# Two residual convolutions in 32x32 tiles: the relu in two halves, and the first two taps bank pair by bank pair

## What is computed

```python
x = x + relu(conv3x3(group_norm(x), kern) + b)
```

## Time and profile before

| | us |
|---|---|
| median of 3 runs | 4687.26 |
| lowest, highest | 4683.33, 4693.34 |
| profiled execution | 4676.86 |
| its span | 4675.1 |
| PE busy in the span | 4587.9 (98%) |
| DVE busy | 2845.1 (61%) |
| ACT busy | 2199.5 (47%) |
| POOL busy | 1265.0 (27%) |
| granted TensorE clock, mean | 0.997 of full |

### The profile page before, as it was taken

How to read it: one execution, slowest core, us unless ns; L and a number is a source line. 1 busy time by engine, 2 the same in 40 slices (tenths; PEclk the granted TensorE clock), 3 DMA queues, 4 the chain that set the end, 5 groups by cost and what they waited for, 6 DMA issues and landing times.

```text
span 4675.1 us, 288889 instructions
## 1 busy us (share of the span) xinstructions
PE 4587.9 (98%) x138240; PEld 2626.0 (56%) x138240; DVE 2845.1 (61%) x3341; ACT 2199.5 (47%) x2242; POOL 1265.0 (27%) x1093
## 2 busy tenths in 40 slices
PE   5999999999999999999999999999999999999999
PEld 3555555555555555555555555555555555555555
DVE  4656656566566566665666656656656666566564
ACT  4454444544445444444454444444544444445442
POOL 3322322323223222232232322322313223223230
PEclk9999999999999999999999999999999999999999
DMA  3333333333333333333333333333333333333323
GB/s 120 108 120 117 124 121 122 118 122 116 122 121 120 118 119 120 123 118 121 122 119 121 121 120 121 120 121 122 120 121 121 120 125 117 121 122 120 121 91 102
DMA packets 542278, 555.71 MB, mean 119 GB/s; under 512 B 16432, under 2 KB 541104, under 8 KB 541104
## 3 DMA queue, kind: packets, MB, share of 16 engines
q1 hardware_dynamic: 541104, 537.22, 35.0%
HBM read 268.72 MB, written 268.44 MB: 115 GB/s over the span
## 4 chain that ended last, share of the span: by engine, by line
PE 94%; issue 3%; ACT 1%; DVE 0%; ACTq 0%; DVEq 0%
PE ps_y L374 35%; PE ps_y L336 34%; PE ps_x L399 12%; PE ps_x L354 10%; PE ps_y L319 2%; PE ps_x L299 1%; ACT relu L457 1%; ACT relu L454 0%; PE ps_x L309 0%; DVE evens L554 0%; DVE result L571 0%; ACTq L452 0%; DVE pixels L586 0%; DVEq L100 0%; ACT evens L465 0%
## 5 line engine op out<-in xcount | busy, mean ns | idle before, releaser
L374 PE MATMUL ps_y<-odds,scaled 32*32 32x512 f32 x49152 | 1766.8, 600 | 7.9 <-issue 2.2
L336 PE MATMUL ps_y<-evens,scaled 32*32 32x512 f32 x49152 | 1745.3, 598 | 23.6 <-ACT evens L465 8.3
L574 DVE TENSOR_TENSOR odds<-ps_x,relu 128x2048 f32<-128x2048 f32 x256 | 586.8, 2292 | 1110.7 <-PE ps_x L354 842.1
L374 PEld LDWEIGHTS ps_y<-odds,scaled 32*32 32x32 f32 x49152 | 808.0, 103 | 794.2 <-issue 376.4
L336 PEld LDWEIGHTS ps_y<-evens,scaled 32*32 32x32 f32 x49152 | 852.8, 103 | 699.8 <-issue 214.0
L457 ACT ACTIVATE relu<-ps_y,bias 128x2048 f32<-128x2048 f32 x256 | 503.8, 1968 | 1094.3 <-PE ps_y L374 942.7
L280 POOL TENSOR_TENSOR fold<-fold,evens 128x1024 f32<-128x1024 f32 x384 | 845.0, 2200 | 597.3 <-DVE evens L561 309.8
L571 DVE TENSOR_TENSOR result<-ps_x,relu 128x2048 f32<-128x2048 f32 x256 | 586.6, 2292 | 636.4 <-PE ps_x L399 439.2
L454 ACT ACTIVATE relu<-ps_y,bias 128x2048 f32<-128x2048 f32 x256 | 503.7, 1968 | 920.8 <-PE ps_y L336 910.6
L354 PE MATMUL ps_x<-evens,constants 32*32 32x512 f32 x16384 | 786.7, 596 | 0.0
L399 PE MATMUL ps_x<-odds,constants 32*32 32x512 f32 x16384 | 776.2, 604 | 0.0
(11 more groups left out here) (49 smaller groups left out, 1266.7 us busy)
## 6 DMA issues: line engine op xcount, KB each, us to landing
out<-pixels SPq DMA_DIRECT2D x512, 512.0 KB, 3.5
raw<-in_x SPq DMA_DIRECT2D x256, 512.0 KB, 3.9
raw<-in_x SPq DMA_DIRECT2D x128, 576.0 KB, 4.1
raw<-in_x SPq DMA_DIRECT2D x128, 448.0 KB, 3.5
parameters<-in_params SPq DMA_DIRECT2D x2, 96.5 KB, 2.0
constants<-in_consts SPq DMA_DIRECT2D x1, 81.0 KB, 2.0
```

The source lines that it names most:

```text
L336: done = nc.tensor.matmul(ps_y[part, r, :], w0[rows, t * Q:(t + 1) * Q], N0[rows, k:k + EACH, i:i + HQ], start=(t == 0), stop=(t == NTAP - ...
L374: done = nc.tensor.matmul(ps_y[Q * r:Q * (r + 1), q, :], w1[p % 2][Q * q:Q * (q + 1), t * Q:(t + 1) * Q], t1[Q * q:Q * (q + 1), k:k + EACH ...
L574: nc.vector.tensor_tensor(T1[p % 2][:, EACH * f:EACH * (f + 1), 1:1 + H].rearrange("p k (r h) -> p r k h", h=HQ), ps_x[:].rearrange("p r ( ...
```

## The change

ACT's relu becomes two ACTIVATEs of two banks each (banks 0 and 1, then 2 and 3), each of which raises `relued` by one; the sums of layer 0 go to eight columns instead of four. All waits for `relued` are counted anew. PE's order in a round is given by `tile_order`: taps 0 and 1 (LEAD = 2) are done on banks 0 and 1, then taps 0 and 1 on banks 2 and 3, then taps 2 to 5 on all four banks in the old order. The wait for the first relu half stands before the first product on banks 0 and 1, that for the second half before the first product on banks 2 and 3. In the first round of layer 0 the wrap products of taps 0 and 1 come together after the lead. `ps_x`, the small products and the adds stay, the adds waiting for both halves.

```diff
@@ -36,7 +37,10 @@
 HALO0, HALO1 = 2 * (QUADS - 1), QUADS
 ODDS_SUM, ODDS_PAD = 1, 2
 EVENS_SUM = 2
+RELUS = 2
+BANKS = QUADS // RELUS
 HOOK_AFTER = 2
+LEAD = 2
 
 
 def freed(f):
@@ -75,6 +79,15 @@
 
 
 MINI = small_products()
+
+
+def tile_order():
+
+    lead = [(t, bank, other) for i in range(RELUS) for t in range(LEAD)
+            for other, bank in itertools.product(range(QUADS), range(BANKS * i, BANKS * (i + 1)))]
+    rest = [(t, bank, other) for t in range(LEAD, NTAP)
+            for other, bank in itertools.product(range(QUADS), range(QUADS))]
+    return lead + rest
 
 
 def norms_before(y, p):
@@ -122,7 +135,7 @@
         ends = sb("ends", [P, HALVES, 2, C])
         zeros = sb("zeros", [P, PAIRS + 2])
         acc = [sb(f"partial{y}", [P, ROUNDS]) for y in range(2)]
-        acc_relu = sb("partial_relu", [P, ROUNDS])
+        acc_relu = sb("partial_relu", [P, ROUNDS * RELUS])
         sums = [sb(f"sums{y}", [P, 2]) for y in range(2)]
         mom = [sb(f"moments{y}", [P, 2]) for y in range(2)]
         center = [mom[y][:, 0:1] for y in range(2)]
@@ -321,24 +334,26 @@
 
             def conv0(p, f):
                 n = round_of(0, p, f)
-                if n:
-                    pe.wait_ge(relued, n)
                 if f == 0:
                     pe.wait_ge(scaled0, p + 1)
                     pe.wait_ge(padded0, p + 1)
                     pe.wait_ge(halo0, HALO0 * (p + 1))
-                for t in range(NTAP):
+                for t, r, q in tile_order():
+                    if t == 0 and q == 0 and r % BANKS == 0 and n:
+                        pe.wait_ge(relued, RELUS * (n - 1) + r // BANKS + 1)
                     side, i = t // TAPS, t % TAPS
-                    for q in range(QUADS):
-                        for r in range(QUADS):
-                            k = SLOTS * q + EACH * f + side
-                            rows, part = slice(Q * r, Q * (r + 1)), slice(Q * q, Q * (q + 1))
-                            done = nc.tensor.matmul(ps_y[part, r, :], w0[rows, t * Q:(t + 1) * Q],
-                                                    N0[rows, k:k + EACH, i:i + HQ], start=(t == 0),
-                                                    stop=(t == NTAP - 1), skip_group_check=True)
-                    if f == 0 and t < TAPS + 1:
+                    k = SLOTS * q + EACH * f + side
+                    rows, part = slice(Q * r, Q * (r + 1)), slice(Q * q, Q * (q + 1))
+                    done = nc.tensor.matmul(ps_y[part, r, :], w0[rows, t * Q:(t + 1) * Q],
+                                            N0[rows, k:k + EACH, i:i + HQ], start=(t == 0),
+                                            stop=(t == NTAP - 1), skip_group_check=True)
+                    last = r == QUADS - 1 and q == QUADS - 1
+                    if last and f == 0 and t == LEAD - 1:
+                        for tap in range(LEAD):
+                            wrap_pair(tap)
+                    if last and f == 0 and LEAD <= t < TAPS + 1:
                         wrap_pair(t)
-                    if t == HOOK_AFTER and f == 0:
+                    if last and t == HOOK_AFTER and f == 0:
                         if n:
                             pe.wait_ge(added, n)
                         bias_product(0, p)
@@ -359,23 +374,22 @@
             def conv1(p, f):
                 n = round_of(1, p, f)
                 t1 = T1[p % 2]
-                pe.wait_ge(relued, n)
                 if f == 0:
                     pe.wait_ge(scaled1, p + 1)
                     pe.wait_ge(padded1, p + 1)
                     pe.wait_ge(added, round_of(0, p, ROUNDS - 1) + 1)
                     pe.wait_ge(halo1, HALO1 * (p + 1))
                 last_mini = -1
-                for t in range(NTAP):
+                for t, q, r in tile_order():
+                    if t == 0 and r == 0 and q % BANKS == 0:
+                        pe.wait_ge(relued, RELUS * (n - 1) + q // BANKS + 1)
                     side, i = t // TAPS, t % TAPS
-                    for r in range(QUADS):
-                        for q in range(QUADS):
-                            k = EACH * f + side
-                            done = nc.tensor.matmul(ps_y[Q * r:Q * (r + 1), q, :],
-                                                    w1[p % 2][Q * q:Q * (q + 1), t * Q:(t + 1) * Q],
-                                                    t1[Q * q:Q * (q + 1), k:k + EACH, HQ * r + i:HQ * (r + 1) + i],
-                                                    start=(t == 0), stop=(t == NTAP - 1))
-                    if t == HOOK_AFTER:
+                    k = EACH * f + side
+                    done = nc.tensor.matmul(ps_y[Q * r:Q * (r + 1), q, :],
+                                            w1[p % 2][Q * q:Q * (q + 1), t * Q:(t + 1) * Q],
+                                            t1[Q * q:Q * (q + 1), k:k + EACH, HQ * r + i:HQ * (r + 1) + i],
+                                            start=(t == 0), stop=(t == NTAP - 1))
+                    if t == HOOK_AFTER and r == QUADS - 1 and q == QUADS - 1:
                         if f == 0:
                             pe.wait_ge(added, n)
                             bias_product(1, p)
@@ -450,12 +464,15 @@
                 act.wait_ge(y_filled, n + 1)
                 if n:
                     act.wait_ge(added, n)
-                if y == 0:
-                    ins = nc.scalar.activation(R[:], ps_y[:], ACT.Relu, bias=bias[:, 0:1],
-                                               accum_out=acc_relu[:, f:f + 1])
-                else:
-                    ins = nc.scalar.activation(R[:], ps_y[:], ACT.Relu, bias=bias[:, 1:2])
-                ins.then_inc(relued, 1)
+                for i in range(RELUS):
+                    banks = slice(BANKS * i, BANKS * (i + 1))
+                    if y == 0:
+                        at = RELUS * f + i
+                        nc.scalar.activation(R[:, banks, :], ps_y[:, banks, :], ACT.Relu, bias=bias[:, 0:1],
+                                             accum_out=acc_relu[:, at:at + 1]).then_inc(relued, 1)
+                    else:
+                        nc.scalar.activation(R[:, banks, :], ps_y[:, banks, :], ACT.Relu,
+                                             bias=bias[:, 1:2]).then_inc(relued, 1)
 
             def pad_evens(p):
                 act.wait_ge(scaled0, p + 1)
@@ -563,7 +580,7 @@
 
             def add(y, p, f):
                 n = round_of(y, p, f)
-                dve.wait_ge(relued, n + 1)
+                dve.wait_ge(relued, RELUS * (n + 1))
                 dve.wait_ge(x_filled, n + 1)
                 if y:
                     if ROUNDS * p + f:
```

More of the change, by code:

```diff
@@ L1 @@
+import itertools
 from contextlib import ExitStack
```

## The result

The changed kernel takes 4734.05 us (median of 4 runs, 4727.59 to 4734.45) against 4685.85 us for the kernel before on the same chip (4 runs). The ratio is 1.0097, with a 95% interval of 1.0079 to 1.0114. So it is slower, as forecast, clear of the noise, but by 1% or 48 us and not by some 500: 0.09 us a round where the prediction had 0.99. The range of 4950 to 5330 us does not hold it.

What follows compares the result with a forecast made beforehand. PE's array, 98% busy, was taken as the bound, hiding most relu waits. Per round 0.14 us won at the start and 1.13 paid for the lead gave +0.99, times 512 rounds 507 us: 5180 us, range 4950 to 5330.

Steps and rivals of the forecast that it cites:

- The lead, 1.13 us in the sum: Taps 0 and 1 done by halves: 1.13 us a round paid because eight tiles rest at a time.
- issue is in order: PE's loads: none is taken past one that waits for its tile, read from 0.33 us of idleness.
- A1: Tap 1 on the eight tiles of banks 0 and 1, predicted at X + 1.07.
- X: Moment when most tiles of tap 0 on banks 0 and 1 start, put at 1574.40.
- B0: Tap 0 on the eight tiles of banks 2 and 3, predicted at X + 1.20, not waiting for A1 to end.
- B1: Tap 1 on banks 2 and 3: first tile at X + 2.08, the others from X + 2.27 to X + 2.39.
- The low end that I gave for the round: Tap 2's two waits pay the 0.19 us pause only once: round grows by 0.80 us, 5087 us.
- The start, 0.14 us in the sum: Round start after the first relu half: 0.14 us a round won, although that half is done 0.85 us earlier.
- X itself is set by the array: Round start: ps_x's second stream at 1573.32 puts it at 1574.40; tiles free from 1573.7 are held up.
- (b): Rival, faster: PE takes loads for resting tiles past a waiting tile; only -0.14 us a round remains, 4605 us; chance 0.06.
- (c): Rival, in between: tap 2's waits overlap better, +0.2 to +0.7 us a round, 4780 to 5035 us; chance 0.08.
- (d): Rival, same: start gain and resting tiles cancel, or the order has no effect; within 0.2% of now; chance 0.02.

Runs made afterwards that it cites:

- kernel with the lead alone: The changed kernel's product order, but the relu in one piece with one wait before the round; 5001.69 us, ratio 1.0669 to the kernel before.
- kernel with half the relu: The kernel before, old order, with the relu taking banks 0 and 1 only and that of banks 2 and 3 left out; 4529.48 us, ratio 0.9663.
- five orders: The change 1.0097; old order 1.0172; lead of one tap 1.0052; taps 2 to 5 by halves 1.0065; all taps by halves, lead of one 1.0100.
- 4552 us kernels: The changed kernel with all taps and ps_x by halves, a lead of one tap and `y_filled` raised per half; 4551.99 us, ratio 0.9713.

## Why the prediction was wrong

**What held.** PE's waits on the relu, 461 us in the list, were not there to be won: they went from 461 to under 20 us and the kernel got slower. The relu halves took 1.11 us, ended within 0.1 us of when they were said to, and cost neither ACT nor DVE anything; no wait on the second half took the place of the first. The clock stayed at 0.997 of full speed. The lead costs more than the start brings: the sign comes from that, by 0.09 us a round.

**The lead, 1.13 us in the sum, is 0.61 by itself.** This failed step is "issue is in order", with the 0.19 us pauses carried over from the old order. The sum put A1 at X + 1.07 with such a pause, B0 at 1.20, the rest of B1 at 2.27 to 2.39 and tap 2 behind it. In the kernel with the lead alone A1 starts at 0.88 without a pause, B0 at 1.07 to 1.18 with one tile at 0.64, before A1, and B1 with the first tiles of tap 2 at 1.93 to 2.09. The sentence that no load is taken while a tile waits rested on one place in one order. With eight tiles in a lot, A1's loads and those of B0 behind them were taken one after another. The low end that I gave for the round took away one pause of 0.19; the real price is 0.52 lower.

By the Trainium skill (TensorE: Matmul & The Clock Gate, "The mechanism") a set of eight tiles takes about as long as one of sixteen. The two more sets of the lead would by that cost some 2 us a round, an estimate from the page's rule and the 1.07 us of a tap. The run shows 0.61: the overlap that the sum allowed is there, and is wider.

**The start, 0.14 us in the sum, is 0.85 us at the loads and 0.31 to 0.52 in time.** This is the other step that failed: "X itself is set by the array", where tiles that are free earlier may start, "but the ones behind them hold the order up". X was taken from the pace of a full stream, 1.07 us a tap, as if the tiles were then busy all the time. They aren't: a tile needs 0.88 of the 1.07, and the rest is the pause. In the kernel with half the relu rounds of 8.0 to 8.4 us follow in layer 0 (medians), below eight taps at 1.07, so part of these pauses is won; that a round's first products run in them is how I read it. The price of a tap in a stream that starts in step was taken for the price of any tap.

**The rivals.** (b), the faster case, named the right two questions, whether loads get past and what the start is worth, and was given 0.06; what happened lies between it and the forecast, below the +0.2 where (c) began. (d), within 0.2% of no change by terms that cancel, was nearest in mechanism: the terms do cancel, to 0.09 us a round, though at 1.0% the time lies outside it, and no rival's span holds it. It got 0.02, since both terms were taken from the same wrong pace, so that their errors, -0.5 for the lead and -0.4 for the start, added up. The Trainium skill's sentence on loads pulled ahead of matmuls in flight (same page, "Part 2: What happens when you issue a matmul") was weighed and turned down on the strength of one idle stretch of 0.33 us; the loads of the lead alone (32 in 0.85 us from 1705.86 on, while the tiles before them were in use) speak for it more than I allowed, and so does the matmul at 0.64. So does a line of the kernel before that the earlier trace rows leaves out:

```profile
1566.27 0.10 PEld L336 LDWEIGHTS ps_y<-evens,scaled 32*32 32x32 f32 x1 [0.21 <-issue]
```

The 32 loads at 1565.81 are all that the first tap has, so by the count this one is for the next tap, taken when the second matmuls began and 0.42 us before the first tile was free. Beyond these, which loads pass which isn't shown by a trace that names no tile.

**What stays open** is why in the old order one load is taken ahead, at 0.46 us, and no other before the first tile is free at 0.88, while a lot of eight tiles isn't held like that; by what path the small products, or the wait that goes with them, make the lead dear; and what the early start would bring if the add didn't hold the rounds with sum products.

## What to carry to other kernels

A pause that repeats with each pass of a loop is part of that order of the work and no constant of the engine; before a new order is priced with it, one run of that order alone is worth more than the sum. If a reader of an accumulator is to overlap with the next round, let it start before the round is over, by a semaphore for each half of the banks: that gave 2.9%, where with the halves released only at the end each of five orders stayed 0.5 to 1.7% slower than the kernel before. Once such a wait is gone, look for the next one in the same rounds: here the add held a quarter of them. And a change of two opposed parts that comes out near zero should be taken apart: here +0.61 and -0.52 us a round stood behind +0.09.

## What was not expected of the hardware

- A tap of 16 tiles took 1.07 us in the kernel before, and less with an early start: whole rounds of eight taps took down to 8.0 us (4529 and 4552 us kernels).
- In the kernel with the lead alone one matmul started 0.61 to 0.64 us into 509 of the 512 rounds, some 0.24 us before products that stand ahead of it in the program (by the count of tiles).
- Sixteen products of 32x2 in the middle of a round cost 0.26 us in the old order and 0.44 to 0.82 us in the changed one, and a further 0.23 us in the round behind them.
- A start that came 0.1 us later, or sooner, moved the changed kernel by +3 and -16 us (+6 and -13 by the ratios), although 256 rounds each were shifted.
